# The last attention's clip moved from the scores to the weights behind the exponential

## What is computed

```python
scale = D ** (-0.5)                     # 16 heads of 8
q = (query @ Wq + bq).reshape(B, Nq, H, D).transpose(0, 2, 1, 3)
k = (key_value @ Wk + bk).reshape(B, Nkv, H, D).transpose(0, 2, 1, 3)
v = (key_value @ Wv + bv).reshape(B, Nkv, H, D).transpose(0, 2, 1, 3)
attn = jnp.einsum('bhqd,bhkd->bhqk', q, k) * scale
attn = jnp.clip(attn, -CLAMP, CLAMP)    # CLAMP = 10000.0
attn = jax.nn.softmax(attn, axis=-1)
attn = jnp.where(jnp.any(jnp.isnan(attn)), 1.0 / Nkv, attn)
x = jnp.einsum('bhqk,bhkd->bqhd', attn, v).reshape(B, Nq, Cq)
return x @ Wo + bo
```

## Time and profile before

| | us |
|---|---|
| median of 3 runs (4526.77 to 4539.6) | 4529.12 |
| span of the profiled execution | 4528.5 |
| last attention's scores, first to last | 3579.7 to 4425.2 |
| PE, DVE, ACT, POOL busy over the span | 3764.9, 2775.7, 2053.0, 1442.9 |

### The profile page before, as it was taken

One profiled execution on the slowest core, in us unless ns is written; L12 is line 12 of the kernel. 1 busy time (PEld: TensorE's weight loads), 2 busy tenths in 40 slices (PEclk: granted clock), 3 DMA queues, 4 the chain that ended last, 5 costly groups with the idle time before them and its releaser, 6 DMA issues. The chain is left out here.

```text
span 4528.5 us, 87018 instructions
## 1 busy us (share of the span) xinstructions
PE 3764.9 (83%) x33054; PEld 2482.9 (55%) x33054; DVE 2775.7 (61%) x3532; ACT 2053.0 (45%) x2923; POOL 1442.9 (32%) x1905
## 2 busy tenths in 40 slices
PE   7389888971828999998999998759957699989996
PEld 7156656651514666664666665347723366656663
DVE  8566556644425555543555552467644799989993
ACT  7156666650202443442333333146422377767762
POOL 0264444403042323222222221012200665656630
PEclk9689999995957999997999999879979699999997
DMA  6167566624522333322223331011000566757640
GB/s 170 39 141 158 129 150 143 149 61 163 205 42 66 90 86 82 83 71 64 70 81 80 85 83 44 9 52 46 15 17 14 125 149 157 159 133 157 149 110 14
DMA packets 197067, 434.65 MB, mean 96 GB/s; under 512 B 45707, under 2 KB 98877, under 8 KB 196588
## 3 DMA queue, kind: packets, MB, share of 16 engines
q1 hardware_dynamic: 122196, 338.87, 29.8%
q0 software_dynamic: 38912, 47.06, 4.9%
q10 hardware_dynamic: 35616, 43.97, 3.6%
HBM read 244.72 MB, written 32.67 MB: 61 GB/s over the span
## 5 line engine op out<-in xcount | busy, mean ns | idle before, releaser
L1446 DVE TENSOR_REDUCE L_mp<-ps 112x2 f32<-112x1000 f32 x384 | 458.1, 1198 | 517.0 <-PE ps L1268 513.4
L1305 PE MATMUL ps<-L_p,L_cn 125*97 125x448 f32 x1536 | 639.2, 538 | 0.0
L1429 ACT ACTIVATE L_p<-ps 125x896 f32<-125x896 f32 x384 | 352.2, 917 | 614.8 <-PE ps L1293 541.3
L2116 ACT ACTIVATE L_p<-L_p 125x896 f32<-125x896 f32 x384 | 364.7, 950 | 228.0 <-DVE L_p L2169 227.4
L2152 DVE TENSOR_REDUCE L_mp<-ps 112x2 f32<-112x1000 f32 x384 | 455.4, 1190 | 6.5 <-PE ps L1929 6.5
L911 ACT ACTIVATE L_p<-ps,rk 125x896 f32<-125x896 f32 x384 | 385.8, 1005 | 161.5 <-PE ps L789 142.5
L2169 DVE SCALAR_TENSOR_TENSOR L_p<-ps,xn 125x896 f32<-125x896 f32 x384 | 414.5, 1081 | 40.5 <-PE ps L1948 29.1
L1291 PE MATMUL ps<-L_qh,L_ch 97*125 97x448 f32 x768 | 386.1, 503 | 14.1 <-DMA L_qh<-L_mc 14.1
L1305 PEld LDWEIGHTS ps<-L_p,L_cn 125*97 125x97 f32 x1536 | 250.4, 163 | 205.8 <-issue 165.9
L1929 PE MATMUL ps<-L_ks,L_qs 96*128 96x500 bf16 x768 | 236.2, 392 | 62.4 <-DVE L_mp L2152 50.6
L1292 PE MATMUL ps<-L_ql,L_ch 96*125 96x448 f32 x768 | 284.5, 370 | 0.0
(11 more groups left out here) (525 smaller groups left out, 7239.1 us busy)
## 6 DMA issues: line engine op xcount, KB each, us to landing
L_ks<-L_k_part SPq DMA_DIRECT2D x288, 375.0 KB, 9.0
L_ks<-L_k_first SPq DMA_DIRECT2D x96, 375.0 KB, 6.2
moe_w<-in_L_w SPq DMA_DIRECT2D x64, 512.0 KB
L_cn<-in_ctxN SPq DMA_DIRECT2D x32, 568.4 KB
cs_ct<-in_ctxT SPq DMA_DIRECT2D x32, 562.5 KB, 4.3
L_raw<-in_ctxT SPq DMA_DIRECT2D x32, 562.5 KB
L_cr<-in_ctxT POOLq DMA_DIRECT2D x32, 562.5 KB, 5.0
L_ch<-in_ctxT POOLq DMA_DIRECT2D x32, 562.5 KB, 4.5
```

Source lines behind the costliest of these rows:

```text
L1305: mm = nc.tensor.matmul(U[:, a, :], CN[s][:, j, :], P[:, n % 2, a * HALF:(a + 1) * HALF], start=(j == 0), stop=(j == KT - 1))
L1429: nc.scalar.activation(two(P[:, n % 2, :]), SB[n % 2], ACT.Exp).then_inc(S["exped"].sem, 1)
L1446: nc.vector.tensor_reduce(mp[:, 2 * k:2 * k + 2], ps[0:TT, bank:bank + 2, 0:500], AX.X, ALU.max).then_inc(S["chunk_maxed"].sem, 1)
L2116: nc.scalar.activation(two(P[0:KP, n % 3, :]), two(P[0:KP, n % 3, :]), ACT.Exp).then_inc(S["exped"], 1)
```

## The change

The exponential now reads the scores straight from PSUM, and the clip comes behind it, on the weights in SBUF: `min` with 1 and `max` with `exp(-64)`, two constants, in place. For one constant to serve as lower bound, the shift is held at or above `64 - clip`. The lower bounds `LB`, their copy, their two DMAs and their transpose go. The tiles of weights go round four places (three of `P` and one of the two that held `LB`, now `spare`), `weigh` comes one step later, the bank is freed by `exped`, and a clip is written in step `k` for tile `k`, no longer for `k + 2`. `copy_sums` comes one step later.

```diff
-    LB = core.xn[:, :].rearrange("p (s n) -> p s n", s=2)
+    spare = core.xn[:, :].rearrange("p (s n) -> p s n", s=2)
+    weights_at = [P[:, 0, :], P[:, 1, :], P[:, 2, :], spare[:, 0, :]]
+    least = float(np.exp(-float(LOWEST)))                 # LOWEST = 64.0
...
             def place_max(b):
                 sp.wait_ge(S["turn_copied"], b.lin(1, 1))
-                sp.dma_start(low[b.r % 2].rearrange("o (t n) -> (o t) n", t=8), LBT[:, :]).then_inc(S["lb_out"], 16)
                 sp.dma_start(QS[b.r % 4][96:99, 0:HQ].rearrange("r (m n) -> r m n", n=2 * NQ), MT[:, :]
                              ).then_inc(S[f"max_in{b.r % 2}"], 16)
-                sp.wait_ge(S["lb_out"], b.lin(16, 16))
-                sp.dma_start(LB[0:KP, b.r % 2, :], low[b.r % 2].to_broadcast([KP, HQ])
-                             ).then_inc(S[f"lb_in{b.r % 2}"], 16)
...
-                op(ST[:, 24:32], nm[:, :], most[:, :], ALU.subtract)
...
-                nc.tensor.transpose(ps[0:8, 5, 128:128 + TT], ST[:, 24:32], core.ident[0:TT, 0:TT]
...
                 if b.turn is not None or b.r or n >= 2:
-                    pe.wait_ge(S["clipped"], b.lin(12, n - 1))
+                    pe.wait_ge(S["exped"], b.lin(12, n - 1))
...
             def weigh(b, j):
-                pe.wait_ge(S["exped"], b.lin(12, j + 1))
+                pe.wait_ge(S["clipped"], b.lin(12, j + 1))
...
-                    weigh(b, k)
+                    if k:
+                        weigh(b, k - 1)
+                    elif (b - 1).there():
+                        weigh(b - 1, KT - 1)
...
-                nc.scalar.activation(LBT[:, :], ps[0:8, 5, 128:128 + TT], ACT.Copy)
...
-                    act.wait_ge(S["clipped"], b.lin(12, n + 1))
-                    nc.scalar.activation(two(P[0:KP, n % 3, :]), two(P[0:KP, n % 3, :]), ACT.Exp
+                    act.wait_ge(S["scored"], b.lin(12, n + 1))
+                    if b.turn is not None or b.r or n >= 4:
+                        act.wait_ge(S["weighed"], b.lin(12, n - 3))
+                    nc.scalar.activation(two(weights_at[n % 4][0:KP, :]), SB[n % 2][0:KP], ACT.Exp
                                          ).then_inc(S["exped"], 1)
...
-                nc.vector.tensor_scalar(mc[:, :], mu[:, :], clip, -clip, ALU.min, ALU.max
+                nc.vector.tensor_scalar(mc[:, :], mu[:, :], clip, LOWEST - clip, ALU.min, ALU.max
...
-                nc.vector.scalar_tensor_tensor(out=two(P[0:KP, n % 3, :]), in0=SB[n % 2][0:KP], scalar=0.0,
-                                               in1=two(LB[0:KP, b.r % 2, :]), op0=ALU.min, op1=ALU.max
-                                               ).then_inc(S["clipped"], 1)
+                dve.wait_ge(S["exped"], b.lin(12, n + 1))
+                nc.vector.tensor_scalar(weights_at[n % 4][0:KP, :], weights_at[n % 4][0:KP, :], 1.0, least,
+                                        ALU.min, ALU.max).then_inc(S["clipped"], 1)
...
-                    if k + 2 < KT:
-                        clip_tile(b, k + 2)
-                    elif (b + 1).there():
-                        clip_tile(b + 1, k + 2 - KT)
+                    clip_tile(b, k)
```

More of the change, by code:

```diff
@@ L1527 @@
     LOOP = 8
+LOWEST = 64.0
 TWO_ONES = float(np.array([0x3F803F80], np.uint32).view(np.float32)[0])
@@ L1536 @@
                 "chunk_scored", "chunk_maxed", "max_found", "max_ready", "parts", "turned", "turn_copied",
-                "max_in0", "max_in1", "lb_out", "lb_in0", "lb_in1", "scored", "clipped", "exped", "weighed",
+                "max_in0", "max_in1", "scored", "clipped", "exped", "weighed",
                 "u_copied", "sums_picked", "sums_widened", "sums_spread", "sums_copied", "sums_inverted", "u_normed", "seen", "projected", "out_copied"]
@@ L1609, in clipped_pass @@
     mp, mu, mc = sb("mp", [TT, 24]), sb("mu", [TT, 8]), sb("mc", [TT, 8])
-    zero, most = sb("zero", [TT, 8]), sb("most", [TT, 8])
-    nm, r1, ST = sb("nm", [TT, 8]), sb("r1", [TT, 8]), sb("st", [TT, 32])
+    zero = sb("zero", [TT, 8])
+    nm, r1, ST = sb("nm", [TT, 8]), sb("r1", [TT, 8]), sb("st", [TT, 24])
     b0, b1 = sb("b0", [TT, 8], BF16), sb("b1", [TT, 8], BF16)
-    MT, LBT = sb("mt", [24, TT], BF16), sb("lbt", [8, TT])
-    low = [nc.dram_tensor(f"{L}_low{s}", (1, HQ), F32).ap() for s in range(2)]
+    MT = sb("mt", [24, TT], BF16)
+    least = float(np.exp(-float(LOWEST)))
     SB = [ps[:, 0:2, 0:HALF], ps[:, 2:4, 0:HALF]]
@@ L1767, in _ @@
             link(nc.gpsimd.memset(zero[:, :], 0.0))
-            link(nc.gpsimd.memset(most[:, :], clip))
             link(nc.gpsimd.memset(ok[:, :], 0.0))
@@ L1799, in max_parts @@
                 op(b0[:, :], zero[:, :], mc[:, :], ALU.subtract)
-                pool.wait_ge(done, b.lin(8, 2))
+                pool.wait_ge(done, b.lin(7, 2))
                 op(r1[:, :], nm[:, :], b0[:, :], ALU.subtract)
                 op(ST[:, 0:8], b0[:, :], zero[:, :], ALU.add)
-                op(ST[:, 24:32], nm[:, :], most[:, :], ALU.subtract)
-                pool.wait_ge(done, b.lin(8, 5))
+                pool.wait_ge(done, b.lin(7, 4))
                 op(b1[:, :], r1[:, :], zero[:, :], ALU.add)
-                pool.wait_ge(done, b.lin(8, 6))
+                pool.wait_ge(done, b.lin(7, 5))
                 op(ST[:, 8:16], b1[:, :], zero[:, :], ALU.add)
@@ L1869, in turn @@
             def turn(b):
-                pe.wait_ge(S["parts"], b.lin(8, 8))
-                nc.tensor.transpose(ps[0:24, 5, 0:TT], ST[:, 0:24], core.ident[0:TT, 0:TT])
-                nc.tensor.transpose(ps[0:8, 5, 128:128 + TT], ST[:, 24:32], core.ident[0:TT, 0:TT]
+                pe.wait_ge(S["parts"], b.lin(7, 7))
+                nc.tensor.transpose(ps[0:24, 5, 0:TT], ST[:, :], core.ident[0:TT, 0:TT]
                                     ).then_inc(S["turned"], 1)
@@ L1961, in weigh @@
                     mm = nc.tensor.matmul(ps[32 * g:32 * g + VW, 4, c:c + 2 * NQ], VS[b.r % 2][:, j, m, :],
-                                          P[0:KP, j % 3, m * 2 * NQ:(m + 1) * 2 * NQ],
+                                          weights_at[j % 4][0:KP, m * 2 * NQ:(m + 1) * 2 * NQ],
                                           start=(j == 0 and m < 4), stop=(j == KT - 1 and m >= 4))
@@ L2017, in _ @@
             last = Eight(None, B - 2)
+            weigh(last + 1, KT - 1)
             pe.wait_ge(*emptied("project", 0, last - 2))
@@ L2103, in body @@
                 for n in range(KT):
-                    if n == 1 and (b - 1).there():
+                    if n == 2 and (b - 1).there():
                         copy_sums(b - 1)
@@ L2143, in make_parts @@
                 dve.wait_ge(S["q_made"], 1)
-                qf, rest = (t[:, :, :].rearrange("p s n -> p (s n)") for t in (P[:, 0:2, :], LB))
+                qf, rest = (t.rearrange("p s n -> p (s n)") for t in (P[:, 0:2, :], spare))
                 link(nc.vector.tensor_scalar(qf.rearrange("p (c n) -> p c n", c=NCH), ps[:, 0:NCH, 0:CH],
@@ L2208, in _ @@
                 chunk_max(first + n // 12, n % 12, n % 3)
-            clip_tile(first, 0)
-            clip_tile(first, 1)
             batches(dve, body)
```

## The result

The changed kernel takes 4654.26 us (median of 4 runs, 4650.92 to 4655.78); beside it, on the same chip, the kernel before took 4534.11 (4 runs). The ratio is 1.0264, with a 95% interval of 1.0248 to 1.028: 2.6% slower. The forecast was 4532, with a range of 4500 to 4551. The profiled span is 4653.1 against 4528.5, at a mean granted clock of 0.889 against 0.904.

The account below looks back on a forecast made before the run. Only steps 4 (even), 5 and 6 (odd) go at DVE's pace, others by PE's work. 14 x 0.59 + 15 x 0.09 = +9.6, less 6.8, is +2.8 on 4529.1: 4532, range 4500 to 4551.

Parts of the forecast that it names:

- A: Even batches: clip 4 goes ahead of POOL's first `rest_of_keys`, later clips are held; +0.59 even, +0.09 odd, 4532; chance 0.35.
- case B: Even batches: POOL goes first, clip 4 held to 2.89, later clips by about 0.9; +1.57 a batch, 4546; chance 0.30.
- the walk: Hand-timed batch from T_3 = 0, tracing clips, maxima and POOL; T_9 comes 0.92 later in even, 0.42 in odd batches.
- The floors: Shortest PE steps: 1.89 from `chunks` 0.60, maximum 1.19 and some 0.10 of hand-over; step 1 falls to 2.27.
- (a) to (c): Clip 1.09 to 0.69; earlier exponential saves 0.33 in step 1; steps 4 to 6 shorten: 0.59 even, 0.76 odd.
- start and end: Outside the key-splitting batches: 3.8 gained at the start, some 3 in the last three batches and tail; 6.8 together.
- the first T_3: At the start, T_3 waits for batch 2's keys by DMA: 3594.8 or so against 3598.56, 3.8 gained.
- The 3580.3 of the forecast: At the start, the time when the scores for DVE's first clip are there, from 3579.75 plus half of 1.65.
- The first maximum of the loop 5 earlier: Sign that the forecast is right: at the start, the loop's first maximum comes some 5 earlier.
- The slow kind: Rival: the new clip takes about 1.0, stays clear of POOL, DVE's pace stays 2.10; 4513; chance 0.05.
- POOL takes turns: Rival: DVE waits at most the rest of one POOL instruction, or POOL slips out of rhythm; 4503; chance 0.25.

Follow-up runs that it names:

- the version with parts first: Changed kernel with POOL's large instructions behind clips, rests 0 and 1 early, and clip 4 waiting for POOL's small instructions on the maxima: 4503.27 us, ratio 0.9932.
- the run with half of the columns: Changed kernel with the clip on only the first 448 of the 896 columns of each step's weights: 4618.14 us, ratio 1.0196.
- the run with one wait: Changed kernel with one wait added on POOL: only the second `rest_of_keys` waits, for the clip of step 4: 4559.44 us, ratio 1.007.

## Why the prediction was wrong

**What failed is the sentence "So the clip waits for the POOL instruction in progress, whole."** The cases A and B priced a hold at 0.6 to 0.9, with DVE let in at the next boundary (A: "held to 4.54, ends 5.23"). Measured: 4.82 through four instructions, 2.87 through three for eight columns, 5.90 through five. The two pairs of the earlier trace rows had a single POOL instruction each, so they could not tell one from many. The third figure there, 3254 for L952, was longer than any one POOL instruction beside it, and I left it unexplained. These are its rows in the trace of before, with the last of POOL's three also by itself, and those of a second case:

```profile
267.27 3.25 DVE L952 TENSOR_SCALAR L_img_q<-L_img_r 96x500 bf16<-96x500 f32 x1
268.01 3.51 POOL L700 TENSOR_TENSOR L_k_part<-L_k_rest,L_k_part 128x500 bf16<-128x500 f32 x3
270.19 1.32 POOL L700 TENSOR_TENSOR L_k_part<-L_k_rest,L_k_part 128x500 bf16<-128x500 f32 x1
...
279.60 1.24 DVE L952 TENSOR_SCALAR L_img_q<-L_img_r 96x500 bf16<-96x500 f32 x1
280.53 1.30 POOL L700 TENSOR_TENSOR L_k_part<-L_k_rest,L_k_part 128x500 bf16<-128x500 f32 x1
```

The first began while POOL issued DMAs, was passed over at the boundary behind the first of the three, and was let in ahead of the third, which took 1.32 for the usual 1.14. The second was let in at the first boundary that it met, ahead of a POOL instruction that took 1.30. So the trace of before had a warning, a hold over more than one instruction, but in both cases DVE was let in before the run was over. Why not in the changed kernel is open. The earlier trace rows showed that the new clip would meet seven in a row. The Trainium skill, SBUF — State Buffer, section Who interferes with whom, says that whoever issues first gets the shared pair for the whole instruction and the other blocks; it says nothing of who is next. The rows do: with the clip already waiting, the same engine again in 62 of 64.

**Also missing: what PE loses behind a hold.** I wrote that `weigh` has 0.5 to 0.6 of room; a hold of 4.8 leaves PE idle, and the granted clock was 0.50 for 6.8 us afterwards. In the even batch the hold's own step costs 3.86 and the next 1.95, of 6.20 in all. **And the other direction**: the walk had POOL's parts wait for one clip (0.58), not for clips still queued. In the odd batches, some 3.9 longer than without the clip, it cost 1.7 to 2.6; most of the rest is the clip held two steps later.

**What held.** The floors: T_1 to T_2 is 2.27, and (a) to (c) give 25.70 and 25.44 a batch for 29 batches; without the clip, and in the version with parts first, it is 25.65 and 25.39. The version with parts first, the fastest with the whole clip, also tests the forecast's start and end. From the first `mu` to the last it takes 812.3, against 836.6 before, by

```profile
L2157 DVE TENSOR_REDUCE L_mu<-L_mp x32: 177/178/180, 3562.6 to 4399.2; 112x8 f32<-112x24 f32 x32
```

in the kernel before and

```profile
L2166 DVE TENSOR_REDUCE L_mu<-L_mp x32: 177/178/180, 3561.4 to 4373.7; 112x8 f32<-112x24 f32 x32
```

in that one: 24.3 less. The two profiled spans, 4528.5 and 4501.8, differ by 26.7, where 19.7 for the batches and 6.8 for start and end were forecast. That the sum is so near is in part luck: the batches gave 0.05 more each than forecast, 21.1 over the 29, and start and end less. The keys' transfer does set the first T_3, as forecast:

```profile
3593.89 1.01 PE L1933 MATMUL ps<-L_ks,L_qs 96*128 96x500 bf16 x2 [6.55 <-DMA L_ks<-L_k_part]
```

This is 0.9 ahead of the 3594.8 forecast; in the changed kernel it is 3601.39, 2.8 behind the kernel before. (The 3580.3 of the forecast is 3580.6 by its own numbers; no term of the sum uses it.) "The first maximum of the loop 5 earlier" cannot be read from these rows, which vary by as much from kernel to kernel (3568.0 in the changed one). The fast clip takes 0.62, where I took 0.69 from the earlier trace rows; by itself that changes nothing, as DVE has room. The formula of the Trainium skill (VectorE: DVE Perf Modes, TRN2 errata) gave 0.53, and is short of the row by 0.09. The same section of the Trainium skill says that this formula is too short for a single instruction and that the fixed part measures some 150 cycles, not 58; by that the clip is an estimate of 0.62, and the trace agrees (617 ns). The slow kind, forecast at 4513 for 1.0 us, measured 4518.54 at 1.08, and "POOL takes turns", at 4503, is what the kernel reaches when it is made to (4503.27). So the prices of these two rivals were right to 6 us; case B's was met in no run. The chance of 0.05 for anything beyond case B was too small.

**What stays open.** Why one and the same queue of POOL instructions lets DVE in when the clip is next behind a maximum and not when it stands waiting, was counted, not explained; not all boundaries follow it (in the changed kernel, with DVE in its maximum and the clip next, POOL's next large instruction went ahead in 17 of 42; in the run with half of the columns, DVE stood waiting and was let in at 15 of 82). Nor was it tried how short a gap on POOL is enough; those made here were 0.56 or longer.

## What to carry to other kernels

Making a DVE instruction cheaper by moving it from PSUM to SBUF can make it collide with POOL. Then count POOL's instructions in a row, not the one beside it: the price can be the whole run, 8 to 10 times the clip itself here, and PE's clock on top. Give POOL's work places (behind the instructions that need the port), let short instructions that someone waits for go ahead of them, and look at what the delay makes late: here the keys' transfer. A maximum that no single neighbour explains, such as 3254 ns, is worth the query before a forecast rests on the median.

## What the runs showed of the hardware

- A `tensor_scalar` of 0.11 us on 112x8 elements was held for 2.87 us in the median; 32 of them, 29 of which were held, made a kernel of 4530 us slower by 130.
- A clip that is only queued behind a running maximum can hold POOL: 0.20 became 1.64, ended by the clip. In the run with one wait it did so at every `third_of_keys` of the batch shown (1.90 in place of 1.11), at no cost to PE.
- A `tensor_reduce` with the same operands is neither held nor does it hold: 1026 to 1089 ns over 384 of them, and POOL's small instructions stay at 0.20 beside it.
- After the 5.7 us of the hold, in which PE was busy for 1.69, the granted clock was at the lower level, 1.2 GHz, for 6.8 us.
